# A wavelet mix on one core: the early unit's edge operand holds the high part twice, GpSimd sends it, and one matmul step stands for two

## The chip, the cores and the metric

The kernel runs on one core of a Trainium2 chip. The metric is device time in microseconds; the time of a kernel is the median of several runs. The five engines of the core (TensorE, VectorE, ScalarE, GpSimd, SyncE) each take their own instructions in order and meet through semaphores. In the profile they are PE (with PEld for its weight loads), DVE, ACT, POOL and SP.

## The reference

`x` has the shape (8, 512, 207, 64): batch, time, node, channel. For every batch, node and channel the 512 time steps go through a three-level wavelet analysis (filters of eight taps), each of the four components is scaled by a weight per channel, the signal is put together again, and a 64x64 projection with a bias and the input itself are added:

```
for _ in range(3): a, d = dwt(a); details.append(d)
coeffs = [a] + details[::-1]
enh = [c * w[i] for i, c in enumerate(coeffs)]      # w[i] per channel
rec = enh[0]
for d in enh[1:]: rec = idwt(rec[:, :d.shape[-1]], d)
return x + rec @ proj_w.T + proj_b
```

All of it is in float32.

## The kernel before

Analysis and synthesis are matrices, so the kernel does three products: analysis along time, projection along channels, synthesis along time. Time is cut into four blocks ("windows") of 128 steps, 0 to 3. Because a filter reaches over the end of a block, a block's synthesis needs, beside its own 128 coefficients, the first 20 coefficients (`HALO_COLS`) of the block behind it: the edge.

The 8x207 nodes are taken 18 at a time into four slots of SBUF. Four pairs of nodes (512 columns) make a group; nine groups make a turn of the four slots, and 23 turns make the 207 groups. The first and the last turn are written out; those between are one hardware loop on each engine. Loads and stores of x are issued by SyncE, a slot's two stores and two later loads together.

For a group, the engines do the following.

- **Analysis** (`analyse_first`, `analyse_second`, L340): TensorE multiplies a pair's x by the analysis matrix into one PSUM tile, `coefs_ps`, which serves all pairs in turn. VectorE scales it into SBUF (`scale_pair`, L602) and so frees the tile. GpSimd adds the seam (`add_seam`, L305). All of this runs one group ahead.
- **Projection** (`project`, L390, and `project_tail`, L400): a block of four pairs goes into one of two PSUM tiles, in the order `ORDER`, which is 2, 3, 0, 1. Projecting block 2 waits for the seam of each pair.
- **Split**: for synthesis the projected values are split in a high part of the fast matmul format and a low part that is the rest. ScalarE copies the high part (`copy_high`, L534), VectorE subtracts (`split_low`, L609), and that frees the PSUM tile. A tail of the last block is transposed by VectorE (`turn_tail`, L620) and split by ScalarE (`copy_tail_high`, L542) and GpSimd (`split_tail`, L309).
- **Edge operand**: `stack_sb` holds, for each unit, the high edge at row 0, three rows of the bias from row 20 on (`BIAS_AT`), and the low edge at row 32, in each half of 64 rows. ScalarE moves the edges (`move_edge`, L552) and the tail (`move_tail`, L565, eight moves).
- **Synthesis** in two units, blocks 2 and 3 (LATE) and blocks 0 and 1 (EARLY): `synthesise_first` and `synthesise_second` do three products (low matrix with high data, high with low, high with high) in two halves, and at the end of the second half come the edge steps, L442 and L444: one with `edge_lo`, one with `edge_hi`. The two matmuls of a step work in two row halves of TensorE at once.
- **Sum**: VectorE adds the result to x (`add_window`, L629).

TensorE's order inside group g is written out by hand:

```
synthesise_second(*behind, LATE);  first_ahead(0)
project(turn, g, 2, ...);  second_ahead(0);  project(turn, g, 3, ...);  project_tail(g)
first_ahead(1);  synthesise_first(*behind, EARLY, [0, 1, 2], False);  second_ahead(1)
synthesise_second(*behind, EARLY);  first_ahead(2)
project(turn, g, 0, ...);  second_ahead(2);  project(turn, g, 1, ...)
synthesise_first(turn, g, LATE, [0], first);  first_ahead(3)
synthesise_first(turn, g, LATE, [1, 2], first);  second_ahead(3)
```

`first_ahead(p)` waits until pair p-1 of the next group has been scaled (`scaled`), `second_ahead(p)` is the other half of pair p. VectorE's order is: the low part of the last block of the group behind, the sums of blocks 2 and 3, scaling pair 0, low parts of blocks 2 and 3, scaling pair 1, the transposes, the sums of blocks 0 and 1, scaling pair 2, the low part of the third block, scaling pair 3. ScalarE's order is: early edges of the group behind (block 2, block 1), high copies of blocks 2 and 3, the late unit's edge, the tail's copy, the eight tail moves, high copies of the third and fourth block. GpSimd's order is: seams 0 and 1, the tail's low part, seams 2 and 3.

Of the kernel before, what the change touches and what calls it, by code (L numbers as in the profile page):

```python
# [34 lines left out]
PAIRS = 4  # L35
# [3 lines left out]

ORDER = [2, 3, 0, 1]  # L40
PLACE = [ORDER.index(w) for w in range(WINDOWS)]
UNITS = [(2, 3), (0, 1)]
LATE, EARLY = 0, 1

HIGH_AT, LOW_AT = 0, QUAD
BIAS_AT = HALO_COLS
BIAS_PARTS = 3

SLOTS = 4
# [47 lines left out]
def constant_matrices():  # L97
# [18 lines left out]
    e = np.stack([synthesis[i][t0:t0 + WINDOW, k] for i, k in half_columns(half + 1)[HALF:]]).astype(np.float32)  # L116
    edge = np.zeros((HALF, 2, WINDOW), np.float32)
    edge[HIGH_AT:HIGH_AT + HALO_COLS, 0] = e
    edge[LOW_AT:LOW_AT + HALO_COLS, 0] = e
    edge[BIAS_AT:BIAS_AT + BIAS_PARTS, 0] = 1.0  # L120
    edge[HIGH_AT:HIGH_AT + HALO_COLS, 1] = e
    return np.concatenate([a, a]), s, np.concatenate([edge, edge]).reshape(2 * HALF, 2 * WINDOW)

# [14 lines left out]
def wavelet_mix(nc, x, comp_w, w_t, bias, analysis_m, synthesis_m, edge_m, out):  # L138
# [11 lines left out]
    with ExitStack() as ctx:  # L150
# [13 lines left out]
        synthesis_lo = sb("synthesis_lo", [WINDOW, WINDOW], fp32r)  # L164
        edge_sb = sb("edge_sb", [2 * HALF, 2, WINDOW])
        edge_hi = sb("edge_hi", [2 * HALF, 2, WINDOW], fp32r)
        edge_lo = sb("edge_lo", [2 * HALF, WINDOW], fp32r)
        w_sb = sb("w_sb", [PAIR, PAIR])
        comp_sb = sb("comp_sb", [PAIR, COMPONENTS])
# [25 lines left out]
        bias_split = sem("bias_split")  # L195
        rest_built = sem("rest_built")
        stacks_set = sem("stacks_set")
        first_loaded = [sem(f"first_loaded{i}") for i in range(3)]
# [11 lines left out]
        tail_lo_copied = sem("tail_lo_copied")  # L210
        edge_moved = {w: sem(f"edge_moved{w}") for w in (1, 2, 3)}
        tail_moved = sem("tail_moved")
        half_synthesised = sem("half_synthesised")
# [4 lines left out]
        FIRST_NODES = [0, 4, 10, SLOT_NODES]  # L218
        EDGE_MOVES = 2
        TAIL_MOVES = 2 * 4  # L220
# [71 lines left out]
        def _(pool):  # L292
# [7 lines left out]
            def add_seam(turn, g, p):  # L300
# [11 lines left out]
            def turn_of(turn, last=False):  # L312
# [12 lines left out]

            for p in range(PAIRS):
                add_seam(0, 0, p)
            turn_of(0)
            with nc.Fori(1, TURNS - 1, engines=(ENG.Pool,), hint_back_edge=True) as turn:
# [4 lines left out]
        def _(pe):  # L334
# [91 lines left out]
            def synthesise_second(turn, g, u):  # L426
# [21 lines left out]
            def turn_of(turn, first=False, last=False):  # L448
                for g in range(GROUPS):
# [24 lines left out]
                    if not start:  # L474
                        synthesise_second(*behind, EARLY)
                    first_ahead(2)
                    project(turn, g, 0, [0, 1, 2, 3], first)
                    second_ahead(2)
                    project(turn, g, 1, [0, 1, 2, 3], first)
                    if start:  # L480
                        pe.wait_ge(lo_built, 2)
                        pe.wait_ge(stacks_set, 16 * STACK_DMAS)
# [18 lines left out]
        def _(act):  # L501
# [18 lines left out]
            for u in range(2):  # L520
                for half in range(2):
                    for part in range(BIAS_PARTS):
                        row = half * HALF + BIAS_AT + part
# [20 lines left out]
            def move_edge(turn, g, w, u, half, first):  # L544

                group = turn * GROUPS + g
                act.wait_ge(lo_copied, group * WINDOWS + (PLACE[w] + 1))
# [21 lines left out]
            def turn_of(turn, first=False):  # L569
                for g in range(GROUPS):  # L570
# [7 lines left out]
                    copy_tail_high(turn, g, first)  # L578
                    move_tail(turn, g, first)
                    copy_high(turn, g, 0, first)  # L580
                    copy_high(turn, g, 1, first)

# [7 lines left out]
        def _(dve):  # L590
# [33 lines left out]
            def add_window(turn, g, w):  # L624
                group = turn * GROUPS + g
                dve.wait_ge(synthesised, group * 2 + (PLACE[w] // 2 + 1))
                cols = x_sb[:, w, g * GROUP:(g + 1) * GROUP].rearrange("t (p q c) -> t q p c", p=PAIRS, q=4)
                rec = synth_ps[PLACE[w] % 2][:, :].rearrange("t (q p c) -> t q p c", p=PAIRS, q=4)
                nc.vector.tensor_tensor(cols, rec, cols, ALU.add).then_inc(summed, 1)  # L629

            def turn_of(turn, first=False, last=False):
                for g in range(GROUPS):
# [11 lines left out]
                    if not (first and g == 0):  # L644
                        split_low(*behind, 1)
                    add_behind(2)
# [8 lines left out]
                    scale_ahead(2)  # L655
                    split_low(turn, g, 0)
                    scale_ahead(3)

            for p in range(PAIRS):
# [15 lines left out]
            turn_of(TURNS - 1, last=True)  # L675
            split_low(TURNS - 1, GROUPS - 1, 1)
            for w in ORDER:
                add_window(TURNS - 1, GROUPS - 1, w)
# [23 lines left out]
```

## Time and profile before

| | us |
|---|---|
| median of 3 runs | 2435.3 |
| lowest and highest run | 2433.97, 2440.68 |
| the profiled execution, its own time | 2432.38 |
| its span, first to last instruction | 2430.5 |
| busy: PE, PEld | 2357.3, 2200.8 |
| busy: ACT, DVE, POOL | 1830.6, 1752.8, 290.8 |

The granted TensorE clock is 0.99 over the span. A matmul's end is modelled in the profile and matmuls overlap, so a busy PE row says that matmuls were in flight, not that they ran at the peak.

### The profile page before, as it was taken

How to read it: one execution, taken by the hardware profiler on the slowest of the kernel's cores; microseconds unless marked ns; L12 is line 12 of the kernel's file. 1: busy time of each engine (PE TensorE's matmuls, PEld its weight loads, DVE VectorE, ACT ScalarE, POOL GpSimd, SP SyncE). 2: the span in 40 equal slices, each digit the busy share in tenths (PEclk: the TensorE clock that was granted, in tenths of full speed). 3: DMA queues.
4: the chain of work that ended last, by engine and by line, in shares of the span. 5: the costliest groups of instructions: out<-in, count | busy, mean ns of one | idle time of the engine just before them, and what ended most of it. 6: DMA issues, size and time to landing. Idle time of an engine off the chain costs nothing.

```text
span 2430.5 us, 85182 instructions
## 1 busy us (share of the span) xinstructions
PE 2357.3 (97%) x33948; PEld 2200.8 (91%) x33948; DVE 1752.8 (72%) x2906; ACT 1830.6 (75%) x3938; POOL 290.8 (12%) x1111
## 2 busy tenths in 40 slices
PE   6999999999999999999999999999999999999997
PEld 5999999999999999999999999999999899999996
DVE  3777767777777777777777776777777777777775
ACT  3777777777777777777777786777777777777776
POOL 2111111111111111111111111111111111111110
PEclk9999999999999999999999999999999999999998
DMA  3446455454455445464464544544454454544542
GB/s 123 157 166 227 157 189 186 175 195 176 185 187 199 170 174 206 162 230 157 157 235 157 217 176 157 194 173 183 189 204 163 174 213 157 210 182 158 215 177 118
DMA packets 106678, 439.38 MB, mean 181 GB/s; under 512 B 6785, under 2 KB 8065, under 8 KB 106370
## 3 DMA queue, kind: packets, MB, share of 16 engines
q1 hardware_dynamic: 105232, 434.13, 47.4%
q8 instruction: 296, 4.85, 0.8%
q10 hardware_dynamic: 1138, 0.30, 0.1%
q14 instruction: 12, 0.10, 0.0%
HBM read 217.33 MB, written 217.06 MB: 179 GB/s over the span
## 4 chain that ended last, share of the span: by engine, by line
PE 96%; issue 2%; DVE 1%; POOL 0%; ACTq 0%; DMA 0%; ACT 0%; DVEq 0%
PE coefs_ps L340 30%; PE proj_ps L390 30%; PE synth_ps L419 11%; PE synth_ps L431 10%; PE synth_ps L442 6%; PE synth_ps L433 3%; PE proj_ps L400 2%; PE synth_ps L421 2%; PE synth_ps L444 2%; POOL scale_sb L296 0%; ACTq L524 0%; DMA comp_sb<-comp_w 0%; DVE coefs_sb L602 0%; DVE proj_lo L609 0%; DVE x_sb L629 0%
## 5 line engine op out<-in xcount | busy, mean ns | idle before, releaser
L340 PEld LDWEIGHTS coefs_ps<-analysis_sb,x_sb 64*128 64x128 f32 x13248 | 956.8, 189 | 120.9 <-DVE coefs_sb L602 63.5
L340 PE MATMUL coefs_ps<-analysis_sb,x_sb 64*128 64x84 f32 x13248 | 1017.3, 271 | 23.6 <-DVE coefs_sb L602 18.1
L390 PE MATMUL proj_ps<-w_sb,coefs_sb 64*128 64x64 f32 x13248 | 878.8, 272 | 8.1 <-issue 7.7
L609 DVE TENSOR_TENSOR proj_lo<-proj_ps,proj_hi 128x512 fp32r<-128x512 f32 x828 | 567.8, 686 | 365.6 <-ACT proj_hi L534 365.6
L390 PEld LDWEIGHTS proj_ps<-w_sb,coefs_sb 64*128 64x128 f32 x13248 | 821.4, 190 | 10.6 <-issue 10.5
L602 DVE TENSOR_TENSOR coefs_sb<-coefs_ps,scale_sb 128x552 f32<-128x552 f32 x828 | 604.7, 730 | 253.3 <-PE coefs_ps L340 237.8
L534 ACT ACTIVATE proj_hi<-proj_ps 128x512 fp32r<-128x512 f32 x828 | 471.9, 596 | 218.3 <-PE proj_ps L400 160.0
L629 DVE TENSOR_TENSOR x_sb<-synth_ps,x_sb 128x512 f32<-128x512 f32 x828 | 531.6, 684 | 44.9 <-PE synth_ps L444 38.5
L552 ACT ACTIVATE stack_sb<-proj_hi 20x512 fp32r<-20x512 f32 x621 | 390.8, 629 | 214.1 <-DVE proj_lo L609 209.0
L305 POOL TENSOR_TENSOR coefs_sb<-coefs_sb 128x20 f32<-128x20 f32 x828 | 187.0, 226 | 1953.7 <-DVE coefs_sb L602 1953.7
L552 ACT ACTIVATE stack_sb<-proj_lo 20x512 fp32r<-20x512 f32 x621 | 390.5, 629 | 15.2
L565 ACT ACTIVATE stack_sb<-tail_hi 20x128 fp32r<-20x128 f32 x828 | 255.1, 308 | 21.8
L565 ACT ACTIVATE stack_sb<-tail_lo 20x128 fp32r<-20x128 f32 x828 | 255.1, 308 | 20.2
L431 PE MATMUL synth_ps<-proj_hi,synthesis_lo 64*128 64x512 f32 x414 | 200.0, 483 | 29.5 <-issue 29.3
L419 PE MATMUL synth_ps<-proj_hi,synthesis_lo 64*128 64x512 f32 x414 | 197.7, 478 | 2.7 <-DVE x_sb L629 2.7
L433 PE MATMUL synth_ps<-proj_hi,synthesis_lo 64*128 64x512 f32 x414 | 199.6, 482 | 0.0
L421 PE MATMUL synth_ps<-proj_hi,synthesis_lo 64*128 64x512 f32 x414 | 198.1, 478 | 0.0
L421 PE MATMUL synth_ps<-proj_lo,synthesis_hi 64*128 64x512 f32 x414 | 179.7, 434 | 0.0
L419 PE MATMUL synth_ps<-proj_lo,synthesis_hi 64*128 64x512 f32 x414 | 179.7, 434 | 0.0
L421 PE MATMUL synth_ps<-proj_hi,synthesis_hi 64*128 64x512 f32 x414 | 163.2, 394 | 0.0
L419 PE MATMUL synth_ps<-proj_hi,synthesis_hi 64*128 64x512 f32 x414 | 163.1, 394 | 0.0
L442 PE MATMUL synth_ps<-stack_sb,edge_lo 64*128 64x512 f32 x414 | 162.3, 392 | 0.3 <-ACT stack_sb L565 0.3
(46 smaller groups left out, 2840.4 us busy)
## 6 DMA issues: line engine op xcount, KB each, us to landing
out<-x_sb SPq DMA_DIRECT2D x184, 1152.0 KB, 6.3
x_sb<-x SPq DMA_DIRECT2D x182, 1152.0 KB, 11.6
x_sb<-x SPq DMA_DIRECT2D x1, 1024.0 KB, 8.5
x_sb<-x SPq DMA_DIRECT2D x1, 768.0 KB, 6.0
x_sb<-x SPq DMA_DIRECT2D x1, 512.0 KB, 4.1
stack_sb<-bias_parts ACTq DMA_DIRECT2D x12, 2.0 KB, 1.7
edge_sb<-edge_m ACTq DMA_DIRECT2D x1, 128.0 KB, 6.0
synthesis_sb<-synthesis_m ACTq DMA_DIRECT2D x1, 64.0 KB, 6.1
```

What stands on the lines that cost most here:

```text
L340: return lambda cols: nc.tensor.matmul(coefs_ps[:, w // PART_WINDOWS, at:at + HALF_COLS], x_sb[half_rows[side], w, cols], analysis_sb[half ...
L390: mm = nc.tensor.matmul(out_cols[:, :, p, :], coefs_of(g, p)[rows, own_cols(w)], w_sb[rows, rows].rearrange("k (h c) -> k h c", h=2), star ...
L419: nc.tensor.matmul(synth_ps[0][:, :], weight[half_rows[0], :], low[half_rows[0], :], start=step == 0, stop=False, skip_group_check=True)
L421: mm = nc.tensor.matmul(synth_ps[1][:, :], weight[half_rows[1], :], high[half_rows[1], :], start=step == 0, stop=False, skip_group_check=True)
L431: nc.tensor.matmul(synth_ps[1][:, :], weight[half_rows[0], :], high[half_rows[0], :], start=False, stop=False, skip_group_check=True)
L442: nc.tensor.matmul(synth_ps[1][:, :], weight[half_rows[0], :], stack_sb[u][half_rows[0], :], start=False, stop=stop, skip_group_check=True)
L534: nc.scalar.activation(proj_hi[w][:, :].rearrange("k (n c) -> k n c", n=2), proj_of(w)[:, :, 0:NODE_COLS], ACT.Copy).then_inc(hi_copied, 1)
L552: nc.scalar.activation(stack_sb[u][rows, :], source[0:HALO_COLS, :].bitcast(fp32), ACT.Copy).then_inc(edge_moved[w], 1)
L565: nc.scalar.activation(stack_sb[LATE][at:at + HALO_COLS, cols], source[q * QUAD:q * QUAD + HALO_COLS, :].bitcast(fp32), ACT.Copy).then_inc ...
L602: nc.vector.tensor_tensor(coefs_of(g, p)[:, 0:PARTS * PART_COLS].rearrange("c (two k) -> c two k", two=PARTS), coefs_ps[:, :, 0:PART_COLS] ...
L609: nc.vector.tensor_tensor(proj_lo[w][:, :].rearrange(by_node, n=2), proj_of(w)[:, :, 0:NODE_COLS], proj_hi[w][:, :].bitcast(fp32).rearrang ...
L629: nc.vector.tensor_tensor(cols, rec, cols, ALU.add).then_inc(summed, 1)
```

## The change

The early unit's two edge steps become one. Its edge operand gets a new layout in each half of 64 rows: high edge at row 0, the high edge again at row 20 (`AGAIN_AT`), the low edge at row 40 (`EARLY_LOW_AT`), the bias from row 60. One weight matrix, `edge_one`, has the high part of the edge matrix at rows 0 and 40, its low part at row 20, and ones at the bias. So the three products of the edge (high with high, low with high, high with low) come out of a single step of 63 rows. `edge_one` is built by VectorE at the start, from a constant that has four kinds (`EDGE_KINDS`) in place of two.

ScalarE still moves the high edge to row 0 for blocks 1 and 2; it no longer moves their low edges. GpSimd sends the high edge to row 20 and the low edge to row 40 by two DMA transfers for each of blocks 2 and 1 (`send_edge`), 20 rows of 2 KB each. GpSimd waits (`await_edge`) until the early unit of the group behind has been synthesised and the block's high and low parts are there. The transfers of block 2 stand between the seams of pairs 2 and 3, those of block 1 behind the seam of pair 3. TensorE waits for both kinds ahead of the early edge step, and ScalarE waits for the transfers of the group before until it copies over their source.

Block 1 is projected ahead of block 0, and is copied and split ahead of it. The late unit keeps its two steps.

```diff
-ORDER = [2, 3, 0, 1]
+ORDER = [2, 3, 1, 0]
...
-BIAS_AT = HALO_COLS
+AGAIN_AT, EARLY_LOW_AT = HALO_COLS, 2 * HALO_COLS
+BIAS_AT = [HALO_COLS, 3 * HALO_COLS]
...
+            def await_edge(turn, g, w, first=False):
+                group = turn * GROUPS + g
+                if not first:
+                    pool.wait_ge(synthesised, group * 2)
+                pool.wait_ge(hi_copied, group * WINDOWS + (PLACE[w] + 1))
+                pool.wait_ge(lo_copied, group * WINDOWS + (PLACE[w] + 1))
+
+            def send_edge(w, half):
+
+                for at, source in ((AGAIN_AT, proj_hi[w]), (EARLY_LOW_AT, proj_lo[w])):
+                    rows = slice(half * HALF + at, half * HALF + at + HALO_COLS)
+                    pool.dma_start(stack_sb[EARLY][rows, :].bitcast(fp32),
+                                   source[0:HALO_COLS, :].bitcast(fp32)).then_inc(edge_sent[w], 16)
...
                     split_tail(turn, g)
+                    await_edge(turn, g, 2, first and g == 0)
                     seam_ahead(2)
+                    send_edge(2, 0)
+                    await_edge(turn, g, 1, first and g == 0)
                     seam_ahead(3)
+                    send_edge(1, 1)
...
                 if u == LATE:
                     pe.wait_ge(tail_moved, (group + 1) * TAIL_MOVES)
-                    pe.wait_ge(edge_moved[3], (group + 1) * EDGE_MOVES)
+                    pe.wait_ge(edge_moved[3], (group + 1) * EDGE_MOVES[3])
+                    edges = [(edge_lo[:, :], False), (edge_hi[:, 0, :], True)]
                 else:
-                    pe.wait_ge(edge_moved[2], (group + 1) * EDGE_MOVES)
-                    pe.wait_ge(edge_moved[1], (group + 1) * EDGE_MOVES)
-                for weight, stop in ((edge_lo[:, :], False), (edge_hi[:, 0, :], True)):
+                    for w in (2, 1):
+                        pe.wait_ge(edge_moved[w], (group + 1) * EDGE_MOVES[w])
+                        pe.wait_ge(edge_sent[w], (group + 1) * EDGE_SENDS)
+                    edges = [(edge_one[:, :], True)]
+                for weight, stop in edges:
...
+                    project(turn, g, 1, [0, 1, 2, 3], first)
+                    second_ahead(2)
                     project(turn, g, 0, [0, 1, 2, 3], first)
-                    second_ahead(2)
-                    project(turn, g, 1, [0, 1, 2, 3], first)
...
                     if w in edge_moved:
-                        act.wait_ge(edge_moved[w], group * EDGE_MOVES)
+                        act.wait_ge(edge_moved[w], group * EDGE_MOVES[w])
+                    if w in edge_sent:
+                        act.wait_ge(edge_sent[w], group * EDGE_SENDS)
...
-                for at, source in ((HIGH_AT, proj_hi[w]), (LOW_AT, proj_lo[w])):
+                for at, source in ((HIGH_AT, proj_hi[w]), (LOW_AT, proj_lo[w]))[0:EDGE_MOVES[w]]:
...
+            nc.vector.tensor_tensor(edge_rest[:, :], edge_sb[:, 3, :], edge_hi[:, 3, :].bitcast(fp32),
+                                    ALU.subtract).then_inc(rest_split, 1)
+            dve.wait_ge(rest_split, 1)
+            nc.vector.tensor_tensor(edge_one[:, :], edge_rest[:, :].bitcast(fp32), edge_hi[:, 2, :].bitcast(fp32),
+                                    ALU.add).then_inc(lo_built, 1)
```

## Rows read from the trace of the kernel before

**Rows 1.** The page: busy time of each engine, and the chain that ended last, by engine.

```profile
PE 2357.3 (97%) x33948; PEld 2200.8 (91%) x33948; DVE 1752.8 (72%) x2906; ACT 1830.6 (75%) x3938; POOL 290.8 (12%) x1111
...
PE 96%; issue 2%; DVE 1%; POOL 0%; ACTq 0%; DMA 0%; ACT 0%; DVEq 0%
```

**Rows 2.** The chain in order of time, one mid-run group: start us, us, what.

```profile
1202.22 0.23 PE synth_ps L442
1202.45 0.41 PE coefs_ps L340 x6
...
1207.88 0.53 PE coefs_ps L340 x8
```

**Rows 3.** Timeline of VectorE, same group: start us, us, operation, idle before and releaser.

```profile
1201.31 0.73 DVE L602 TENSOR_TENSOR coefs_sb<-coefs_ps,scale_sb 128x552 f32<-128x552 f32 x1 [0.24 <-PE coefs_ps L340]
1201.96 0.63 DVE L620 STREAM_TRANSPOSE tail_sb<-proj_ps 64x128 f32<-64x128 f32 x2
...
1206.34 0.69 DVE L609 TENSOR_TENSOR proj_lo<-proj_ps,proj_hi 128x512 fp32r<-128x512 f32 x1 [1.35 <-ACT proj_hi L534]
1206.95 0.72 DVE L602 TENSOR_TENSOR coefs_sb<-coefs_ps,scale_sb 128x552 f32<-128x552 f32 x1
```

**Rows 4.** Timeline of TensorE's weight loads, same group.

```profile
1201.84 0.18 PEld L444 LDWEIGHTS synth_ps<-stack_sb,edge_hi 64*128 64x128 f32 x1
1202.10 0.60 PEld L340 LDWEIGHTS coefs_ps<-analysis_sb,x_sb 64*128 64x128 f32 x8
...
1207.72 0.52 PEld L340 LDWEIGHTS coefs_ps<-analysis_sb,x_sb 64*128 64x128 f32 x8 [0.28 <-DVE coefs_sb L602]
...
1208.16 0.98 PEld L390 LDWEIGHTS proj_ps<-w_sb,coefs_sb 64*128 64x128 f32 x16
```

**Rows 5.** Waits over the run: who waited for whom, us, times, longest us.

```profile
PEld coefs_ps L340 <- DVE coefs_sb L602: 63.5, 181, 11.0
```

**Rows 6.** Timeline of ScalarE, same group and the start of the next.

```profile
1202.71 0.31 ACT L542 ACTIVATE tail_hi<-tail_sb 128x128 fp32r<-128x128 f32 x1 [0.32 <-DVE tail_sb L620]
...
1204.38 1.31 ACT L565 ACTIVATE stack_sb<-tail_lo 20x128 fp32r<-20x128 f32 x4
1205.71 1.09 ACT L534 ACTIVATE proj_hi<-proj_ps 128x512 fp32r<-128x512 f32 x2
...
1209.61 0.60 ACT L534 ACTIVATE proj_hi<-proj_ps 128x512 fp32r<-128x512 f32 x1
...
1213.89 0.31 ACT L542 ACTIVATE tail_hi<-tail_sb 128x128 fp32r<-128x128 f32 x1 [0.31 <-DVE tail_sb L620]
```

**Rows 7.** Timelines of VectorE and ScalarE in the first turn.

```profile
66.67 0.63 DVE L620 STREAM_TRANSPOSE tail_sb<-proj_ps 64x128 f32<-64x128 f32 x2
...
67.33 0.31 ACT L542 ACTIVATE tail_hi<-tail_sb 128x128 fp32r<-128x128 f32 x1 [0.22 <-DVE tail_sb L620]
...
78.44 0.31 ACT L542 ACTIVATE tail_hi<-tail_sb 128x128 fp32r<-128x128 f32 x1 [0.23 <-DVE tail_sb L620]
```

**Rows 8.** The page's groups of instructions: busy us, mean ns, idle before.

```profile
L552 ACT ACTIVATE stack_sb<-proj_lo 20x512 fp32r<-20x512 f32 x621 | 390.5, 629 | 15.2
```

**Rows 9.** Timeline of GpSimd, same group: the seams of pairs 2 and 3.

```profile
1205.07 0.23 POOL L305 TENSOR_TENSOR coefs_sb<-coefs_sb 128x20 f32<-128x20 f32 x1 [1.52 <-DVE coefs_sb L602]
1207.75 0.23 POOL L305 TENSOR_TENSOR coefs_sb<-coefs_sb 128x20 f32<-128x20 f32 x1 [2.46 <-DVE coefs_sb L602]
```

**Rows 10.** ScalarE's DMA issues at the start, and median us to landing.

```profile
30.21 7.64 ACTq L524 DMA_DIRECT2D stack_sb<-bias_parts  x12
...
stack_sb<-bias_parts ACTq DMA_DIRECT2D x12, 2.0 KB, 1.7
edge_sb<-edge_m ACTq DMA_DIRECT2D x1, 128.0 KB, 6.0
```

**Rows 11.** Busy time by window; the DMA engines' share stands behind the clock.

```profile
1190.00:1290.00 100.00, 98.42 (x1440) 91.91 (x1438) 74.07 (x123) 78.25 (x170) 12.00 (x44) 1.00 0.48 183
```

**Rows 12.** Timelines of VectorE and ScalarE at the start.

```profile
27.87 0.34 DVE L664 TENSOR_TENSOR edge_lo<-edge_sb,edge_hi 128x128 fp32r<-128x128 f32 x1
28.13 0.67 DVE L667 TENSOR_TENSOR bias_rest<-bias_sb,bias_parts 1x512 f32<-1x512 f32 x1
...
37.90 1.08 ACT L534 ACTIVATE proj_hi<-proj_ps 128x512 fp32r<-128x512 f32 x2 [8.43 <-issue]
```

More of the change, by code:

```diff
@@ L45 @@
 HIGH_AT, LOW_AT = 0, QUAD
-BIAS_AT = HALO_COLS
+AGAIN_AT, EARLY_LOW_AT = HALO_COLS, 2 * HALO_COLS
+BIAS_AT = [HALO_COLS, 3 * HALO_COLS]
 BIAS_PARTS = 3
+EDGE_KINDS = 4
 SLOTS = 4
@@ L116, in constant_matrices @@
     e = np.stack([synthesis[i][t0:t0 + WINDOW, k] for i, k in half_columns(half + 1)[HALF:]]).astype(np.float32)
-    edge = np.zeros((HALF, 2, WINDOW), np.float32)
+    edge = np.zeros((HALF, EDGE_KINDS, WINDOW), np.float32)
     edge[HIGH_AT:HIGH_AT + HALO_COLS, 0] = e
     edge[LOW_AT:LOW_AT + HALO_COLS, 0] = e
-    edge[BIAS_AT:BIAS_AT + BIAS_PARTS, 0] = 1.0
+    edge[BIAS_AT[LATE]:BIAS_AT[LATE] + BIAS_PARTS, 0] = 1.0
     edge[HIGH_AT:HIGH_AT + HALO_COLS, 1] = e
-    return np.concatenate([a, a]), s, np.concatenate([edge, edge]).reshape(2 * HALF, 2 * WINDOW)
+    edge[HIGH_AT:HIGH_AT + HALO_COLS, 2] = e
+    edge[EARLY_LOW_AT:EARLY_LOW_AT + HALO_COLS, 2] = e
+    edge[BIAS_AT[EARLY]:BIAS_AT[EARLY] + BIAS_PARTS, 2] = 1.0
+    edge[AGAIN_AT:AGAIN_AT + HALO_COLS, 3] = e
+    return np.concatenate([a, a]), s, np.concatenate([edge, edge]).reshape(2 * HALF, EDGE_KINDS * WINDOW)
 def component_runs():
@@ L164, in wavelet_mix @@
         synthesis_lo = sb("synthesis_lo", [WINDOW, WINDOW], fp32r)
-        edge_sb = sb("edge_sb", [2 * HALF, 2, WINDOW])
-        edge_hi = sb("edge_hi", [2 * HALF, 2, WINDOW], fp32r)
+        edge_sb = sb("edge_sb", [2 * HALF, EDGE_KINDS, WINDOW])
+        edge_hi = sb("edge_hi", [2 * HALF, EDGE_KINDS, WINDOW], fp32r)
         edge_lo = sb("edge_lo", [2 * HALF, WINDOW], fp32r)
+        edge_rest = sb("edge_rest", [2 * HALF, WINDOW], fp32r)
+        edge_one = sb("edge_one", [2 * HALF, WINDOW], fp32r)
         w_sb = sb("w_sb", [PAIR, PAIR])
@@ L196, in wavelet_mix @@
         rest_built = sem("rest_built")
+        rest_split = sem("rest_split")
         stacks_set = sem("stacks_set")
@@ L211, in wavelet_mix @@
         edge_moved = {w: sem(f"edge_moved{w}") for w in (1, 2, 3)}
+        edge_sent = {w: sem(f"edge_sent{w}") for w in (1, 2)}
         tail_moved = sem("tail_moved")
@@ L218, in wavelet_mix @@
         FIRST_NODES = [0, 4, 10, SLOT_NODES]
-        EDGE_MOVES = 2
+        EDGE_MOVES = {1: 1, 2: 1, 3: 2}
+        EDGE_SENDS = 2 * 16
         TAIL_MOVES = 2 * 4
@@ L310, in split_tail, with turn_of @@
                                         ALU.subtract).then_inc(tail_lo_copied, 1)
-            def turn_of(turn, last=False):
+            def turn_of(turn, first=False, last=False):
                 for g in range(GROUPS):
@@ L322, in turn_of @@
                     split_tail(turn, g)
+                    await_edge(turn, g, 2, first and g == 0)
                     seam_ahead(2)
+                    send_edge(2, 0)
+                    await_edge(turn, g, 1, first and g == 0)
                     seam_ahead(3)
+                    send_edge(1, 1)
             for p in range(PAIRS):
                 add_seam(0, 0, p)
-            turn_of(0)
+            turn_of(0, first=True)
             with nc.Fori(1, TURNS - 1, engines=(ENG.Pool,), hint_back_edge=True) as turn:
@@ L522, in _ @@
                     for part in range(BIAS_PARTS):
-                        row = half * HALF + BIAS_AT + part
+                        row = half * HALF + BIAS_AT[u] + part
                         act.dma_start(stack_sb[u][row:row + 1, :].bitcast(fp32),
@@ L546, in move_edge @@
                 group = turn * GROUPS + g
-                act.wait_ge(lo_copied, group * WINDOWS + (PLACE[w] + 1))
+                act.wait_ge(hi_copied, group * WINDOWS + (PLACE[w] + 1))
+                if EDGE_MOVES[w] == 2:
+                    act.wait_ge(lo_copied, group * WINDOWS + (PLACE[w] + 1))
                 if not (first and g == 0):
                     act.wait_ge(synthesised, group * 2 + (u - 1))
-                for at, source in ((HIGH_AT, proj_hi[w]), (LOW_AT, proj_lo[w])):
+                for at, source in ((HIGH_AT, proj_hi[w]), (LOW_AT, proj_lo[w]))[0:EDGE_MOVES[w]]:
                     rows = slice(half * HALF + at, half * HALF + at + HALO_COLS)
@@ L579, in turn_of @@
                     move_tail(turn, g, first)
+                    copy_high(turn, g, 1, first)
                     copy_high(turn, g, 0, first)
-                    copy_high(turn, g, 1, first)
             turn_of(0, first=True)
@@ L627, in add_window @@
                 cols = x_sb[:, w, g * GROUP:(g + 1) * GROUP].rearrange("t (p q c) -> t q p c", p=PAIRS, q=4)
-                rec = synth_ps[PLACE[w] % 2][:, :].rearrange("t (q p c) -> t q p c", p=PAIRS, q=4)
+                rec = synth_ps[w % 2][:, :].rearrange("t (q p c) -> t q p c", p=PAIRS, q=4)
                 nc.vector.tensor_tensor(cols, rec, cols, ALU.add).then_inc(summed, 1)
@@ L644, in turn_of @@
                     if not (first and g == 0):
-                        split_low(*behind, 1)
+                        split_low(*behind, 0)
                     add_behind(2)
@@ L655, in turn_of @@
                     scale_ahead(2)
-                    split_low(turn, g, 0)
+                    split_low(turn, g, 1)
                     scale_ahead(3)
@@ L675, in _ @@
             turn_of(TURNS - 1, last=True)
-            split_low(TURNS - 1, GROUPS - 1, 1)
-            for w in ORDER:
+            split_low(TURNS - 1, GROUPS - 1, 0)
+            for w in (2, 3, 0, 1):
                 add_window(TURNS - 1, GROUPS - 1, w)
```

2 lines of the change are left out of this document (1 added, 1 removed).

## Prediction

> **What bounds the kernel now.** I read the page first. TensorE is busy for 97% of the span and its weight loads for 91%, and the chain that ended last is TensorE for 96% of its length [rows 1]. Read that way, whatever leaves TensorE leaves the time. The page cannot show whether TensorE, while it looks busy, keeps its own pace or arrives just behind somebody else. So next I read one group of steps in the middle of the run, engine by engine.
>
> In the chain of waits, one edge step takes 0.23 us (its two matmuls, L442 and L444, run side by side in the two row halves), and analysis steps of eight matmuls follow [rows 2]. The analysis step behind the early unit's edge steps takes 0.41 us; the one behind the late unit's edge steps, which is the same work, takes 0.53 us. So 0.12 us per group at the second place is waiting that is booked as TensorE.
>
> The timeline of VectorE and of the weight loads says for whom [rows 3, 4]. Scaling pair 1 (L602) starts at 1201.31, as soon as analysis has finished that pair, and ends at 1202.04. The first weight load of the next analysis (L340, which overwrites the same PSUM) starts at 1202.10. The load ahead of it, of the second early edge step, had started at 1201.84, and edge loads follow one another every 0.23 us, so without VectorE this load could have come at 1202.07. **Gate one**: TensorE leaves the early unit 0.06 us after VectorE lets it, and only 0.03 us after it could have left by itself. Scaling pair 3 ends at 1207.67, and the weight load behind it comes at 1207.72 after 0.28 us of idle. **Gate two**: there TensorE already waits. Over the run, weight loads of analysis wait 63.5 us for VectorE, 181 times [rows 5].
>
> What makes pair 3 so late is a chain through two engines without a hole [rows 3, 6]: scaling pair 1 at 1201.31; the two transposes 1201.96 to 1202.59; ScalarE's copy of the tail 1202.71; eight tail moves until 1205.69; the high copies from 1205.71, of which the first releases VectorE's low part (L609) at 1206.34; scaling pair 3 from 1206.95 to 1207.67. That is 6.41 us from scaling pair 1 to the weight load at gate two, and nothing in it is TensorE. The copy of the tail comes every 11.18 us (1202.71, 1213.89); the other 4.77 us is TensorE's work from gate two to the end of pair 1's analysis.
>
> The first turn proves that this chain sets the pace [rows 7]. Its instructions are written out, and the tail copy starts 0.03 us after the transposes end (67.30 to 67.33) instead of 0.12 us. The link is 0.09 us shorter, and the group takes 11.11 us instead of 11.18, although TensorE's work is the same.
>
> **The change, part by part.**
>
> *The edge step that goes.* One of two steps in the early unit: 0.23 us per group, 207 groups, 47 us of TensorE work. But it lies between the end of pair 1's analysis and gate one. VectorE needs 0.73 us for pair 1 plus 0.06 us to be seen, whatever TensorE does meanwhile. Four steps instead of five let TensorE arrive 0.23 us earlier, and it then waits 0.20 us for the same scaling. That leaves 0.03 us at most at gate one, and there is nothing left of it at gate two, since the 6.41 us start at pair 1's scaling and do not contain the step. Behind it, the adds of the early unit's blocks may start earlier, but VectorE is in its transposes until 1202.59. Sum: 0 us.
>
> *ScalarE's work that goes.* Two moves of 20x512 from the low parts per group, 0.63 us each by the page (L552, 621 calls [rows 8], of which 414 go): 260 us of ScalarE. They lie behind the high copies (1205.71, two in 1.09 us) and ahead of the next block 2 copy at 1209.61 [rows 6], hence outside the 6.41 us. The copy of block 2 can start some 0.3 us earlier, when its projection ends; its low part still queues behind scaling pair 0 on VectorE. Sum: 0. The eight tail moves, which are in the chain, stay.
>
> *Block 1 ahead of block 0.* Same matmuls, same copies, same PSUM buffers, so each place in the three queues holds a step of the same length. The high copy behind the tail moves now has more waits in front of it; all are for things of the group before, and ScalarE's sequencer can take them during 2.6 us of tail moves. Sum: 0.
>
> *GpSimd's transfers.* Four per group, 20 rows of 2 KB each. GpSimd finishes pair 2's seam at 1205.30 and starts pair 3's at 1207.75 [rows 9], 2.45 us of idle into which block 2's two go; block 1's two come behind pair 3's seam, at 1207.98. No row has a transfer issued by GpSimd, so I bound the cost by ScalarE's. Call c the time that one issue holds the queue and L the time from the start of its issue to landing. ScalarE's twelve issues took 7.64 us, so c = 0.64 from below; from above c = 1.7, the whole way to landing of one of those. L runs from 1.7 us (2 KB, nothing else in flight) to 6.0 us (128 KB while the first loads of x run) [rows 10]. I take c = 1.0 and L = 3: more than the quiet row, because the DMA engines are busy 0.48 of the time in mid-run [rows 11], and far under 6.0, because that transfer had six others in front of it on its own queue.
>
> Three steps are queued behind these transfers. (1) Pair 3's seam, for which the next projection of block 2 waits: its weight loads start at 1208.16 and reach pair 3 after three quarters of 0.98 us [rows 4], at 1208.9. The seam must start by 1208.6, so two issues may take 3.3 us; c up to 1.6 is hidden. (2) The next group's block 2 copy at 1209.61, which must not overwrite a source in flight: 1205.30 + c + L = 1209.3. Hidden, with more room behind it. (3) The early edge step itself. Its first weight load of before is 0.23 us ahead of 1201.84 and comes again 11.18 us later, at 1212.8, and gate one forgives another 0.2 us: 1213.0. The last transfer lands at 1207.98 + c + L = 1212.0 for my values. **The condition is c + L up to 5.0 us**; at 4.0 it is hidden with 1.0 us to spare. If that cover goes, every microsecond late costs 207 us, for TensorE stands with the edge step, the next analysis and block 1's projection behind it. TensorE's two further waits are taken ahead of the matmuls and cost nothing while gate one holds.
>
> The Trainium skill ("DMA: Bandwidth & Descriptors", section "Anatomy of one DMA — SWDGE (gpsimd) path") puts a fixed cost of about 2.0 us on a transfer sent by GpSimd, nearly all of it completion. By that, the last one would land at some 1211.0, and the result would be the same, no change; no row of this trace shows such a transfer.
>
> *Start and end.* Two more VectorE operations of 0.34 us (as L664) stand ahead of the bias parts, and behind those wait ScalarE's twelve issues and then the first high copies at 37.90 [rows 10, 12]: +0.7 us once. The wider constant and its copy end long before. The end loses one step: nothing worth a term.
>
> Sum against the profiled execution's own 2432.4 us (span 2430.5 and 1.9 around it): 2432.4 + 0.7 = 2433.1. That execution lies 2.9 us under the median of 2435.3, so 2436 us for a median.
>
> **The rivals.**
>
> *TensorE sets the pace* (faster). Then 47 us go: 2388 us. For it speak 97% and 91% [rows 1]; against it, both gates and the first turn [rows 3, 4, 7]. The Trainium skill ("Perfetto Trace Analysis", section "Identifying the Most-Contended Engine") would have the engine with the highest occupancy optimized first, TensorE being judged by its weight loads. By that rule 2388 us comes out; the measured waits at the gates speak against it here. A smaller gain is possible if ScalarE's sequencer places its register work otherwise: the 0.09 us ahead of the tail copy is worth 17 us over the 198 looped groups. Together 0.10.
>
> *The transfers come late* (slower). It decides from c + L = 5.0 us, or from c = 1.6 at the seam. With c = 1 and L = 6.0, the row taken under load, the edge step is 2.0 us late: 414 us if in every group (2850 us), some 200 us if only while the DMA engines are busy, 0.48 of the time (2635 us). Half a microsecond late in each group gives 104 us: 2540 us. For it: the program issues a slot's stores and the next loads together, so x moves in bursts, and no row has GpSimd issuing beside one. Against it: a queue of its own, 20 rows, and 1.0 us to spare. Chance 0.35.
>
> *No change* as summed: 0.55.
>
> **The numbers.** A measurement of this kernel tells 0.3%, some 7 us, from no change. The likeliest case gives 2436 us and by itself 2429 to 2443. The range goes down to 2425, which leaves out the larger half of the gains (some 0.07), and up to 2535, transfers half a microsecond late, which leaves out the worse third of that case (0.12). Faster 0.10, same 0.55, slower 0.35.
>
> **What would show it.** Right: the early unit has one edge step, and the weight load of the next analysis now idles some 0.2 us for VectorE, in nearly every group, still 0.06 us behind scaling pair 1; the tail copy still comes every 11.18 us; waits of analysis for VectorE grow from 63.5 us by some 40. Wrong to the fast side: a period near 10.95 us. Wrong to the slow side: TensorE's edge load released by a transfer, or block 2's projection by the seam, and a period that varies with x's bursts.

## The result, and the profile after

The changed kernel takes 3158.7 us (3147.9 to 3164.9, 4 runs) beside 2436.1 us (2433.97 to 2440.68, 4 runs) of the kernel before: a ratio of 1.295, with an interval of 1.291 to 1.299. That is 723 us slower. The forecast was no change, 2436 us, with a range up to 2535 us; the time lies far above it. The profiled execution took 3147.9 us, with a span of 3146.1 us.

The page of the changed kernel: busy time, the chain by engine, two groups of instructions, and the edge transfers (KB each, median us from issue to landing).

```profile
PE 2737.5 (87%) x33534; PEld 2529.9 (80%) x33534; DVE 1748.3 (56%) x2908; ACT 1570.7 (50%) x3524; POOL 684.0 (22%) x1939
...
PE 53%; DMA 25%; issue 8%; ACT 7%; DVE 5%; POOL 2%; ACTq 1%; DVEq 0%; POOLq 0%
...
L475 PE MATMUL synth_ps<-stack_sb,edge_one 64*128 64x512 f32 x207 | 111.5, 539 | 365.7 <-DMA stack_sb<-proj_lo 365.7
...
L330 POOL DMA_DIRECT2D stack_sb<-proj_hi x414 | 209.4, 506 | 23.6 <-issue 20.6
...
stack_sb<-proj_hi POOLq DMA_DIRECT2D x414, 40.0 KB, 1.9
stack_sb<-proj_lo POOLq DMA_DIRECT2D x414, 40.0 KB, 2.8
```

Beside [rows 1], a quarter of the chain is now a DMA, and the early edge step (L475) stands 365.7 us for it. The busy time of TensorE has grown by 380 us (2357.3 to 2737.5) although it has 414 matmuls less. So there are two losses: TensorE waits, and afterwards the same work takes longer. The medians of 1.9 and 2.8 us show nothing wrong: a median cannot show that four in ten are very late.

The waits of the changed kernel (us, times, longest):

```profile
ACT proj_hi L569 <- DMA stack_sb<-proj_lo: 463.7, 90, 7.4
...
PE synth_ps L475 <- DMA stack_sb<-proj_lo: 365.7, 90, 4.9
...
PEld coefs_ps L370 <- DVE coefs_sb L639: 86.6, 212, 11.0
```

Ninety waits of 4.06 us on average, in 207 groups. The program has 23 turns of four slots, so x moves in some 92 bursts: nearly every burst makes one group late. The timeline shows one of them, and the group ahead of it, which is on time:

```profile
1489.04 0.18 PEld L475 LDWEIGHTS synth_ps<-stack_sb,edge_one 64*128 64x128 f32 x1
1489.53 0.52 PEld L370 LDWEIGHTS coefs_ps<-analysis_sb,x_sb 64*128 64x128 f32 x8 [0.30 <-DVE coefs_sb L639]
...
1491.37 0.90 SPq L279 DMA_DIRECT2D out<-x_sb  x2
1492.31 2.34 SPq L275 DMA_DIRECT2D x_sb<-x  x2
...
1492.58 0.51 POOL L330 DMA_DIRECT2D stack_sb<-proj_hi  x1
...
1495.35 0.51 POOL L330 DMA_DIRECT2D stack_sb<-proj_hi  x1
1495.85 0.51 POOL L330 DMA_DIRECT2D stack_sb<-proj_lo  x1
...
1504.64 0.76 PE L475 MATMUL synth_ps<-stack_sb,edge_one 64*128 64x512 f32 x1 [3.97 <-DMA stack_sb<-proj_lo]
...
1505.98 1.90 PE L420 MATMUL proj_ps<-w_sb,coefs_sb 64*128 64x64 f32 x16
...
1515.47 1.06 PE L420 MATMUL proj_ps<-w_sb,coefs_sb 64*128 64x64 f32 x16
```

At 1489.53 gate one stands as forecast: behind the single edge step the weight load idles for VectorE. From 1491.37 SyncE issues two stores and two loads of x. The four edge transfers follow; the last, sent at 1495.85, lands at 1504.50 (the chain of waits has 8.65 us for it), and TensorE has stood 3.97 us. After that sixteen projection matmuls take 1.90 us; ten microseconds later they take 1.06 us. Two views of the same stretch say why the transfer is late and why the matmuls are slow. The DMA view, first between the sends and the first edge packet, then over the four sends of this burst, then over the next four, which meet no burst:

```profile
DMA packets 434, 1.93 MB, mean 393 GB/s; under 512 B 16, under 2 KB 16, under 8 KB 434
...
q1 hardware_dynamic: 434, 1.93, 102.9%
...
x_sb<-x SPq DMA_DIRECT2D x2, 1152.0 KB, 13.6
stack_sb<-proj_hi POOLq DMA_DIRECT2D x2, 40.0 KB, 7.2
stack_sb<-proj_lo POOLq DMA_DIRECT2D x2, 40.0 KB, 8.4
...
stack_sb<-proj_hi POOLq DMA_DIRECT2D x2, 40.0 KB, 1.8
stack_sb<-proj_lo POOLq DMA_DIRECT2D x2, 40.0 KB, 1.9
```

In the 4.9 us from 1492.60 to 1497.50 all 434 packets are of x's queue, q1, and none is of the queue of GpSimd's transfers, q0. (The view counts one row of x, 4.6 KB, as a packet.) The same transfer lands after 1.8 us in the quiet and after 7 to 9 us in a burst. Over the run a quarter lands within 1.83 us, half within 1.95, three quarters within 7.33, and the slowest in 9.52; only 62 of the 828 lie between 2.5 and 6 us.

The windows of that stretch (us, busy of PE, PEld, DVE, ACT, POOL, then granted clock, DMA share, GB/s):

```profile
1496.00:1500.00 4.00, 4.00 (x66) 3.87 (x66) 1.63 (x3) 0.00 (x0) 0.58 (x2) 1.00 1.00 291
1500.00:1504.00 4.00, 0.67 (x6) 0.19 (x2) 2.09 (x4) 1.78 (x4) 0.08 (x1) 1.00 1.03 352
1504.00:1508.00 4.00, 3.36 (x30) 3.33 (x31) 1.67 (x4) 3.41 (x11) 0.60 (x2) 0.54 0.55 218
1508.00:1512.00 4.00, 4.00 (x36) 3.89 (x36) 1.33 (x2) 1.99 (x4) 1.17 (x3) 0.50 0.10 21
1512.00:1516.00 4.00, 4.00 (x40) 3.62 (x38) 2.05 (x4) 0.38 (x1) 1.17 (x3) 0.68 0.06 14
1516.00:1520.00 4.00, 4.00 (x64) 3.85 (x64) 2.81 (x5) 1.61 (x3) 0.23 (x1) 1.00 0.05 10
```

TensorE is granted 1.00 (2.4 GHz) until it has stood for 4 us; then 0.50 (1.2 GHz) for some ten microseconds, in which it does 36 matmuls per 4 us and not 64. Over the whole run the clock is 0.845, before it was 0.99. As only these two levels are granted, that makes some 975 us at half clock ((1 − 0.845) / 0.5 of 3146.1 us), against some 49 us before.

### The profile page after: what moved, and what is told of

Read it like the earlier page. It is cut to its first block, busy times and chain, and to the rows that moved or that the text cites. A ratio compares the mean times of both kernels' runs of the same rounds, so it can differ in the third digit from the quotient of the medians.

```text
span 3146.1 us, 86067 instructions
## 1 busy us (share of the span) xinstructions
PE 2737.5 (87%) x33534; PEld 2529.9 (80%) x33534; DVE 1748.3 (56%) x2908; ACT 1570.7 (50%) x3524; POOL 684.0 (22%) x1939
## 4 chain that ended last, share of the span: by engine, by line
PE 53%; DMA 25%; issue 8%; ACT 7%; DVE 5%; POOL 2%; ACTq 1%; DVEq 0%; POOLq 0%
DMA stack_sb<-proj_lo 25%; PE proj_ps L420 18%; PE coefs_ps L370 18%; PE synth_ps L449 7%; ACT stack_sb L602 5%; PE synth_ps L461 4%; PE synth_ps L475 4%; DVE coefs_sb L639 2%; ACT proj_hi L569 2%; DVE tail_sb L657 2%; PE proj_ps L430 1%; ACT tail_hi L577 1%; POOL stack_sb L330 1%; PE synth_ps L451 1%; POOL coefs_sb L317 1%
## 5 line engine op out<-in xcount | busy, mean ns | idle before, releaser
L370 PEld LDWEIGHTS coefs_ps<-analysis_sb,x_sb 64*128 64x128 f32 x13248 | 1146.9, 220 | 154.0 <-DVE coefs_sb L639 86.6
L370 PE MATMUL coefs_ps<-analysis_sb,x_sb 64*128 64x84 f32 x13248 | 1184.1, 302 | 27.2 <-DVE coefs_sb L639 22.0
L420 PE MATMUL proj_ps<-w_sb,coefs_sb 64*128 64x64 f32 x13248 | 1028.6, 302 | 4.9 <-POOL coefs_sb L317 4.9
L420 PEld LDWEIGHTS proj_ps<-w_sb,coefs_sb 64*128 64x128 f32 x13248 | 975.9, 220 | 5.3 <-POOL coefs_sb L317 5.1
L475 PE MATMUL synth_ps<-stack_sb,edge_one 64*128 64x512 f32 x207 | 111.5, 539 | 365.7 <-DMA stack_sb<-proj_lo 365.7
L475 PEld LDWEIGHTS synth_ps<-stack_sb,edge_one 64*128 64x128 f32 x207 | 46.0, 222 | 406.0 <-issue 402.4
L449 PE MATMUL synth_ps<-proj_hi,synthesis_lo 64*128 64x512 f32 x414 | 224.1, 541 | 1.5 <-DVE x_sb L666 1.5
L451 PE MATMUL synth_ps<-proj_hi,synthesis_lo 64*128 64x512 f32 x414 | 224.1, 541 | 0.0
L461 PE MATMUL synth_ps<-proj_hi,synthesis_lo 64*128 64x512 f32 x414 | 219.0, 529 | 0.2
L463 PE MATMUL synth_ps<-proj_hi,synthesis_lo 64*128 64x512 f32 x414 | 218.8, 529 | 0.0
L330 POOL DMA_DIRECT2D stack_sb<-proj_hi x414 | 209.4, 506 | 23.6 <-issue 20.6
L330 POOL DMA_DIRECT2D stack_sb<-proj_lo x414 | 209.3, 506 | 0.0
L449 PE MATMUL synth_ps<-proj_lo,synthesis_hi 64*128 64x512 f32 x414 | 205.9, 497 | 0.0
L451 PE MATMUL synth_ps<-proj_lo,synthesis_hi 64*128 64x512 f32 x414 | 205.8, 497 | 0.0
```

The costliest lines, as they stand in the source:

```text
L330: pool.dma_start(stack_sb[EARLY][rows, :].bitcast(fp32), source[0:HALO_COLS, :].bitcast(fp32)).then_inc(edge_sent[w], 16)
L370: return lambda cols: nc.tensor.matmul(coefs_ps[:, w // PART_WINDOWS, at:at + HALF_COLS], x_sb[half_rows[side], w, cols], analysis_sb[half ...
L420: mm = nc.tensor.matmul(out_cols[:, :, p, :], coefs_of(g, p)[rows, own_cols(w)], w_sb[rows, rows].rearrange("k (h c) -> k h c", h=2), star ...
L449: nc.tensor.matmul(synth_ps[0][:, :], weight[half_rows[0], :], low[half_rows[0], :], start=step == 0, stop=False, skip_group_check=True)
L451: mm = nc.tensor.matmul(synth_ps[1][:, :], weight[half_rows[1], :], high[half_rows[1], :], start=step == 0, stop=False, skip_group_check=True)
```

## The experiments

**Theory A**: the transfers come late beside x; TensorE's wait for them, and the clock that it loses by it, are the loss. The step itself is worth nothing, because of the gates. **Rivals**: the block order; costs of sending that need nobody's wait; the queue or engine that sends; ScalarE's new waits for the transfers. Group times below are the distances between the first transposes of successive groups in the trace; nine groups make a turn, and the last of the nine holds the jump back of the hardware loop.

**Block order alone** (the kernel before):

```diff
-ORDER = [2, 3, 0, 1]
+ORDER = [2, 3, 1, 0]
...
-                    project(turn, g, 0, [0, 1, 2, 3], first)
+                    project(turn, g, 1, [0, 1, 2, 3], first)
                     second_ahead(2)
-                    project(turn, g, 1, [0, 1, 2, 3], first)
+                    project(turn, g, 0, [0, 1, 2, 3], first)
```

> The kernel before with one part of the change alone: block 1 projected, copied and split ahead of block 0. Theory A: 2436 us, within 8. Theory B, as far as it blames the order: 2500 us or more.

Measured: 2436.6 us, ratio 0.999 (0.997 to 1.001), groups of 11.19 us. The order costs nothing.

**Light x** (the changed kernel):

```diff
                 for dram, slot in halves(slot_views(k, x_view)):
+                    if k >= SLOTS:
+                        dram, slot = dram[:, :, 0:CHANNELS], slot[:, :, 0:CHANNELS]
```

> The changed kernel complete with all its waits, but after the first four slots SyncE moves one node of eighteen per slot, in loads and stores (so most of x is neither fetched nor written). Theory A: every transfer of GpSimd lands in about 1.8 us, no waits for them, 2436 us within 10. Theory B: the loss stays, 2900 us or more.

Measured: 2385.2 us, ratio 0.977 (0.973 to 0.982). The DMA and wait views of this run:

```profile
stack_sb<-proj_hi POOLq DMA_DIRECT2D x414, 40.0 KB, 1.8
...
PEld coefs_ps L373 <- DVE coefs_sb L642: 133.7, 363, 11.1
```

Everything else in place, the loss is gone with x's bulk: 0.5% of the transfers take over 5 us, and groups are 11.19 us. So x's bulk makes them late. The 51 us under the expectation come nearly all from the turn boundary, the ninth group: 11.2 to 11.9 us (mean 11.6), where the kernel before takes mostly 13.0 to 13.5 (mean 13.8); over 22 turns that is 48 us. Gate one now shows as forecast: analysis waits 133.7 us for VectorE, 70 us more than in [rows 5].

**Light x in the kernel before** (the same edit):

> The kernel before with x cut as in the light run (after four slots one node of eighteen per slot moves; most of x is neither fetched nor written). The light run of the changed kernel took 2385 us. Theory A (with nothing late, one edge step or two is the same, because the gates behind pair 1 and pair 3 set the pace): 2385 us within 8, the same group of 11.18 us. Theory C (the merged step gained its 47 us there): 2430 us.

Measured: 2372.6 us, ratio 0.976 (0.973 to 0.979), groups of 11.18 us, boundary 11.35 to 11.85. So with light x the change gains none of the 47 us. (2385.2 beside 2372.6 says little of a cost: the two runs were compared with the kernel before at different times, and it then took 2441.5 and 2432.7 us.) The traces of these two runs show where the 0.23 us go. From the last early edge load to the projection behind the next analysis, TensorE's weight loads take 0.92 us with one step and 0.78 with two; behind the late unit, where both kernels have two steps, they take 0.99 and 0.89 (medians). Gate one takes back 0.14 us and gate two 0.10.

**x in eight pieces** (the changed kernel, 288 KB each):

```diff
-        SLOT_DMAS = 2
+        SLOT_DMAS = 8
...
+                return [(dram[:, w:w + 1, :], slot[:, w:w + 1, :]) for w in range(WINDOWS) for dram, slot in parts]
```

> The changed kernel with all its work; SyncE cuts each slot's loads and stores into eight transfers of 288 KB instead of two of 1152 KB, issued at the same points. Theory A in the form that a DMA engine serves queues in turn, one whole transfer's share at a time: the landing beside a burst falls from 7 to 9 us to 2.5 to 4 us, and the time to 2440 to 2600 us. Theory A in the form that whatever was issued first goes first: landing and time stay, 3100 us or more.

Measured: 2573.8 us, ratio 1.054 (1.048 to 1.059). In its waits the edge step waits little, and the first matmul of a turn much:

```profile
PE synth_ps L462 <- issue: 72.2, 20, 4.4
...
PE synth_ps L476 <- DMA stack_sb<-proj_lo: 24.8, 28, 3.1
```

In smaller pieces, x lets the transfers through earlier (medians 3.0 and 3.8 us, 7.9% over 5 us), and most groups take 11.2 to 12 us. The boundary takes mostly 15.5 to 21 us (median 19.4). What that is, the next two tell.

**Eight pieces in the kernel before** (the same edit):

> The kernel before with x cut into eight transfers of 288 KB per slot and direction, all of it moved. With the changed kernel these pieces took 2574 us, of which 6 to 7 us at each of 22 turn boundaries, where TensorE waited for instructions. If the pieces themselves cost the boundary: 2560 to 2585 us. If GpSimd's transfers do: 2436 us, within 10.

Measured: 2498.9 us, ratio 1.027 (1.023 to 1.030), groups of 11.18 us, boundary 13 to 20. The pieces cost 66 us by themselves (the kernel before took 2432.7 us in that comparison), GpSimd's transfers another 75 (2573.8 less 2498.9): neither expectation was right, it is some of each.

**Transfers that nobody waits for** (the changed kernel):

```diff
-                    pool.dma_start(stack_sb[EARLY][rows, :].bitcast(fp32),
-                                   source[0:HALO_COLS, :].bitcast(fp32)).then_inc(edge_sent[w], 16)
+                    pool.dma_start(spare_sb[1][rows, :],
+                                   spare_sb[0][0:HALO_COLS, :]).then_inc(edge_sent[w], 16)
...
-                        pe.wait_ge(edge_sent[w], (group + 1) * EDGE_SENDS)
...
-                    if w in edge_sent:
-                        act.wait_ge(edge_sent[w], group * EDGE_SENDS)
```

> The changed kernel with the same four transfers per group, but from a constant tile into a spare tile; TensorE and ScalarE do not wait for them (GpSimd waits for its own of the group before), so the early unit's edge leaves out its two low-order products. Theory A (all of the loss is that transfers land late behind the bursts of x, and TensorE and ScalarE wait for them): 2436 us, within 10, a group every 11.18 us. Theory B (GpSimd's issues or the extra traffic cost by themselves): at least 2600 us. Theory C (the merged step is worth its 0.23 us per group once nothing waits): 2390 us.

Measured: 2495.2 us, ratio 1.026 (1.022 to 1.029). Groups take 11.18 us, as before; the excess of 62 us lies at the boundaries, 15.6 to 20 us there:

```profile
PE synth_ps L465 <- issue: 64.1, 20, 3.9
```

Before, the same wait was 29.3 us in 20. So in this run some 60 us are the sending's own: the transfers' traffic lengthens the jump back of the loop. They can't be taken off the 723 us, though. The changed kernel's own trace has no such stop: at the first matmul of a turn (L461) TensorE never waits for "issue", and the ninth groups, all of which are late ones, take 16.7 us, no more than other late groups (medians 16.7 to 17.9). There, as far as the trace tells, the whole loss hangs on the waits.

**Constant source** (the changed kernel, real operand):

```diff
-                                   source[0:HALO_COLS, :].bitcast(fp32)).then_inc(edge_sent[w], 16)
+                                   spare_sb[0:HALO_COLS, :]).then_inc(edge_sent[w], 16)
...
-                    if w in edge_sent:
-                        act.wait_ge(edge_sent[w], group * EDGE_SENDS)
```

> The changed kernel with the transfers taken from a constant tile of zeros into the real edge operand, so ScalarE's copies need not wait for them while TensorE's early edge step still does (the edge leaves out its two low-order products). Theory A: the two waits share the loss, and TensorE's alone still gives 2700 to 3000 us. Rival E (ScalarE's wait, which holds up block 2 and with it the whole chain, is what costs): 2500 to 2560 us, as in the scratch run.

Measured: 3148.8 us, ratio 1.294 (1.288 to 1.300):

```profile
PE synth_ps L477 <- DMA stack_sb<-spare_sb: 364.5, 90, 4.9
```

TensorE's wait alone gives the whole loss. ScalarE's 463.7 us, the larger row in the view of waits, cost nothing that shows (10 us less without them): that rival falls.

**ScalarE sends** (the changed kernel):

```diff
+                for at, source in ((AGAIN_AT, proj_hi[w]), (EARLY_LOW_AT, proj_lo[w])):
+                    rows = slice(half * HALF + at, half * HALF + at + HALO_COLS)
+                    act.dma_start(stack_sb[EARLY][rows, :].bitcast(fp32),
+                                  source[0:HALO_COLS, :].bitcast(fp32)).then_inc(edge_sent[w], 16)
```

> The changed kernel complete, but ScalarE issues the four transfers (behind its two high copies) instead of GpSimd. Theory A (a small transfer waits in the shared DMA engines behind the bursts of x, whoever sends it): landing about 1.7 us when quiet and 6 us or more beside a burst, 2850 to 3300 us. Rival D (it is GpSimd's own queue, whose descriptors a program writes, that is slow beside other traffic): landing under 3 us throughout, under 2600 us.

Measured: 3168.4 us, ratio 1.302 (1.296 to 1.307):

```profile
PE synth_ps L471 <- DMA stack_sb<-proj_lo: 381.4, 91, 5.0
```

The same wait on another engine's queue: GpSimd is not to blame. (The edit shows the added lines; GpSimd's sends go.)

**ScalarE's order** (the kernel before). The gates themselves, by an order that makes scaling pair 3 earlier:

```diff
-                    move_tail(turn, g, first)
+                    move_tail(turn, g, first, 0)
                     copy_high(turn, g, 0, first)
+                    move_tail(turn, g, first, 1)
                     copy_high(turn, g, 1, first)
```

> The kernel before with one move: ScalarE copies the third block's high part between its four high and its four low tail moves, not behind all eight. Theory A (the chain from scaling pair 1 through ScalarE to scaling pair 3 sets the pace): pair 3 is scaled as soon as its analysis ends, TensorE loses the 0.12 us of waiting per group, 11.18 becomes 11.03 to 11.07 us, 2405 to 2412 us. Rival (TensorE sets the pace): 2436 us.

Measured: 2423.1 us, ratio 0.994 (0.991 to 0.997), groups of 11.07 to 11.08 us. Gate two was real and its chain set the pace; without it TensorE does at 11.08. The saving was 0.11 us a group, which makes some 22 us in 207; the total shows 0.6%, 10 to 14 us, less than A expected. Of the rest, 10 us are at the jump back, where the weight loads waited 42.5 us in all and before 32.3. This version is a little faster than the kernel before, and so than both.

**Gate one alone** (idle transfers as above, with that order of ScalarE):

> The changed kernel with its transfers sent from a constant to a spare tile, where nobody but GpSimd's next send waits for them (so the two parts of the early edge that they carried are left out of the sum), and with ScalarE's new order: the third block's high part is copied between the four high and the four low tail moves. That order takes gate two away (in the kernel before it gave groups of 11.07 to 11.08 us), TensorE's order is as in the changed kernel, so gate one stands. Theory A (gate one alone hides the step: TensorE arrives 0.23 us earlier and waits 0.20 us for scaling pair 1): groups of 11.04 to 11.08 us, weight loads of analysis waiting some 0.2 us for VectorE in every group, about 2482 us with the 62 us that the idle transfers cost at the turn boundaries. Rival (with gate two gone the step counts): groups of 10.85 us and about 2440 us.

Measured: 2492.8 us, ratio 1.025 (1.021 to 1.029), groups of 10.98 to 11.07 us, median 10.99 (with two steps and the same order of ScalarE: 11.08). Between the two expectations, nearer to A: of the step's 0.23 us, 0.09 arrive and 0.14 are hidden by gate one, which is seen in the weight loads:

```profile
1225.16 0.18 PEld L478 LDWEIGHTS synth_ps<-stack_sb,edge_one 64*128 64x128 f32 x1
...
1225.66 0.52 PEld L374 LDWEIGHTS coefs_ps<-analysis_sb,x_sb 64*128 64x128 f32 x8 [0.28 <-DVE coefs_sb L643]
```

Most of the 0.09 us, of which the prediction allowed 0.03, can be placed. The first load of analysis now comes 0.48 us behind the edge load ahead of it, where it came 0.25 us behind with two steps and the same order of ScalarE, so the wait takes back the whole step. But the eight loads behind that wait then take 0.44 us and not 0.51 (medians), and so 0.07 us arrive. The saving is not in the total: boundaries took up to 20.7 us.

**Both gates out of the way.** TensorE projects the third block ahead of `first_ahead(2)` and half of the fourth behind it, once with the idle transfers and the single step, once in the kernel before with two steps; ScalarE's order is the new one in both. The cut is from the first of the two; in the second, blocks 0 and 1 change places:

```diff
-                    first_ahead(2)
                     project(turn, g, 1, [0, 1, 2, 3], first)
+                    first_ahead(2)
+                    project(turn, g, 0, [0, 1], first)
                     second_ahead(2)
-                    project(turn, g, 0, [0, 1, 2, 3], first)
+                    project(turn, g, 0, [2, 3], first)
```

> The scratch run's kernel (nobody waits for the transfers, one early edge step, 2495 us) with both gates moved: ScalarE copies the third block's high part between its high and low tail moves, and TensorE projects the third block ahead of pair 2's first half and splits the fourth block's projection around its second half. Theory A (the step was worth nothing only because of the gates): the group falls from 11.18 to about 10.85 us, 2420 to 2435 us. Rival (the step is worth nothing anyway): not under 11.03 us a group, 2465 us or more.

> The kernel before with the same two moves of ScalarE's and TensorE's order and both edge steps. Theory A: TensorE's own work now sets the pace, 11.03 to 11.08 us a group, 2405 to 2425 us, hence 0.2 us a group more than the run with one edge step. Rival (the new order alone shortens the group): 10.85 us here too, under 2385 us.

Measured: 2517.2 us, ratio 1.036 (1.031 to 1.042), groups of 11.23; and 2471.5 us, ratio 1.015 (1.012 to 1.019), groups of 11.46. By itself the first lies where its rival put it, and the second above both of its levels, because the order made a new gate: pair 3's analysis now waits for scaling pair 2, in both kernels alike (the first row is of the single step, the second of two):

```profile
1207.33 0.53 PEld L374 LDWEIGHTS coefs_ps<-analysis_sb,x_sb 64*128 64x128 f32 x8 [0.42 <-DVE coefs_sb L644]
...
1202.43 0.52 PEld L340 LDWEIGHTS coefs_ps<-analysis_sb,x_sb 64*128 64x128 f32 x8 [0.43 <-DVE coefs_sb L604]
```

The difference of the two, 11.46 less 11.23, is 0.23 us, the length of the step. They also differ in the block order and the idle transfers, which changed no group's time in the runs above. So the step is worth its full length when neither of the old gates covers it; no run shows that as a gain in the total.

## Why the prediction was wrong, point by point

- **L, the way from issue to landing, taken as 3 us: the step that failed.** I weighed the 6.0 us row down because that transfer stood behind six others on its own queue, counted "a queue of its own, 20 rows" for the change, and raised the quiet 1.7 us only by the mean DMA share of 0.48. But the sends meet a burst whole, with a DMA share of 1.00, and there a transfer takes 7 to 9.5 us, more than the upper bound of 6.0. On ScalarE's queue the edge step stands as long (381.4 us in 91). The Trainium skill ("DMA: Bandwidth & Descriptors", section "Queues, rings and completion order") has each DMA engine go round the queues and switch at packet boundaries, a packet there being typically 9 to 17 descriptors. The 4.9 us with 434 rows of x alone don't speak against that: they are 27 rows for each of the 16 engines, and one transfer of x has 16 (1152 KB in rows of 4.6 KB), so that a packet of that size is a transfer's whole share. With pieces of 288 KB, 4 rows to an engine, the edges did land sooner, at 3.0 and 3.8 us. By that reading, a queue of its own gives a place in the round and not a short wait; no run tests it further.
- **c, the hold of one issue: 1.0 us taken, 0.51 measured.** Projection waited for a seam once, for 5.1 us at the end of the run, and otherwise never, as summed.
- **The condition, c + L up to 5.0 us: right.** In the group shown it is 1504.50 − 1495.35 = 9.15 us, 4.15 over; TensorE stood 3.97.
- **The price of a late transfer: too small.** The rival named the mechanism and the place, at 2.0 us for each late group. Each cost 4.06 us of standing, 366 us in all, and what is left of the 723 us, 4.0 us for each ((723 − 366) / 90), goes with the half clock, which had no term at all. The rival's share, 0.48 of the groups, is near the measured 90 of 207 (0.43) by chance: it was the busy share of the DMA engines, while in fact each of some 92 bursts makes one group late.
- **The ends of the turns: no term.** Where nobody waits for the transfers, they cost some 60 us at the jump back; the sum had nothing there. In the changed kernel that stop doesn't appear.
- **Gates, block order, ScalarE's work at nothing: right.** Without late transfers groups take 11.18 to 11.19 us; the waits of analysis for VectorE grow by 63 to 70 us where 40 were expected; block order is 0 within 0.3%. That the chain through ScalarE sets the pace, which the prediction took as proved by the first turn, is shown by ScalarE's order (11.18 to 11.08 us). At gate one 0.07 to 0.09 us of the step get through and not 0.03, and gate two then takes them. TensorE as the pace, the faster rival, is refuted by the pair with light x: 47 us less work, and no gain.

## What to carry to other kernels

A small transfer that an engine waits for every few microseconds doesn't belong beside bursts of bulk loads: bound its landing by the burst's length, not by its own size, and look at the spread of landings, for the median hides it. A wait of some microseconds on TensorE costs more than its length, since the matmuls behind it run at half clock for a while. And before an operation is removed from the busiest engine, look for what that engine waits for just behind it; here moving one copy on ScalarE (0.6%) was worth more than a whole TensorE step.

## What the runs showed of the hardware that was not expected

The turn's end depends on x's traffic: the ninth group takes 11.35 to 11.85 us with light x, some 13.4 in the kernel before, and up to 20 with GpSimd's transfers or eight pieces. The trace's records of the instruction queue show how. Where TensorE stops at the jump, the stop ends 1.7 us (median) after a 16 KB instruction packet does, in every kernel that has it; the changed kernel has none. That packet starts 1.4 us before TensorE stops in the kernel before (a wait of 1.3 us, median of 25), but 0.2 us after it with the idle transfers (3.0 us, median of 21), and with light x no stop is longer than 0.6 us. So instructions seem to queue behind x as the edges do; no run held only the instructions back.
